# Last batch of the first layer: taken in two halves from the output sums on, one-hot pieces moved behind its rows, landing waits of the stores ahead removed

## The reference, cut to what matters

```python
x = x + 0.5 * L0_ffn(layernorm(x))    # x @ W_base + b, plus the top 2 of 8 low-rank experts, gates by softmax
x = x + L0_attn(layernorm(x))         # 16 heads of 16, LoRA on q, k, v and o
x = x + 0.5 * L0_ffn(layernorm(x))
x = x + 0.5 * L1_ffn(layernorm(x))    # 32 experts, 4 given per token, silu(g) * u, down
x = x + L1_attn(layernorm(x))         # causal, low-rank q and kv, rope
x = x + 0.5 * L1_ffn(layernorm(x))
```

## Time and profile before

| | us |
|---|---|
| median of 3 runs | 1463.39 |
| the profiled execution, its own time | 1460.13 |
| its span, first to last instruction | 1458.3 |
| PE busy | 1262.3 (87%) |
| DVE busy | 952.2 (65%) |
| ACT busy | 670.3 (46%) |
| POOL busy | 491.1 (34%) |

### The profile page before, as it was taken

The page is one execution under the profiler, slowest core; times in us unless marked ns, Lnnn a source line. Parts: engine busy times, 40 slices in busy tenths (PEclk is TensorE's granted clock), DMA queues, the critical chain, the costliest instruction groups (busy, mean ns, idle before and its releaser), DMA issues.

```text
span 1458.3 us, 22406 instructions
## 1 busy us (share of the span) xinstructions
PE 1262.3 (87%) x6657; PEld 824.8 (57%) x6658; DVE 952.2 (65%) x2794; ACT 670.3 (46%) x1700; POOL 491.1 (34%) x493
## 2 busy tenths in 40 slices
PE   6879888898888399998879898889889997799997
PEld 4554243343325388887646455556546655678886
DVE  6796758777778422224698979887897794133334
ACT  2205655556573055553345444553554453255550
POOL 3054040053123645552211211351153143455550
PEclk8989999999999699999999999999999999799999
DMA  8537443065313266544011100020000102355647
GB/s 287 104 36 122 182 87 44 1 120 185 137 37 149 98 230 202 193 154 170 15 44 30 29 1 1 12 105 1 8 33 18 59 33 94 127 189 183 205 138 303
DMA packets 79120, 151.89 MB, mean 104 GB/s; under 512 B 11677, under 2 KB 60254, under 8 KB 75422
## 3 DMA queue, kind: packets, MB, share of 16 engines
q1 hardware_dynamic: 63310, 108.59, 25.8%
q0 software_dynamic: 15264, 41.70, 8.0%
q10 hardware_dynamic: 432, 0.17, 0.0%
HBM read 85.29 MB, written 64.75 MB: 103 GB/s over the span
## 4 chain that ended last, share of the span: by engine, by line
PE 54%; DVE 27%; ACT 6%; issue 6%; POOL 3%; DMA 3%; SPq 0%; DVEq 0%; ACTq 0%; POOLq 0%
PE m_psG L1276 12%; PE m_psY L1292 6%; DVE a_t L1733 5%; DVE a_mx L924 4%; PE a_psA L1490 3%; DVE a_nb L1741 3%; PE a_psO L482 3%; POOL rows_dram L167 3%; PE m_psX L1267 3%; PE a_psU L1469 3%; ACT a_pr L1600 2%; PE a_psU L457 2%; PE a_psU L1478 2%; PE a_psO L1513 2%; DVE a_q L1729 2%
## 5 line engine op out<-in xcount | busy, mean ns | idle before, releaser
L167 POOL DMA_INDIRECT outs_dram<-m_ys,dest x190 | 181.9, 958 | 156.0 <-ACT m_ys L1194 150.8
L1600 ACT ACTIVATE a_pr<-a_psA,a_nb 128x512 f32<-128x512 f32 (+3 forms) x256 | 132.7, 525 | 216.0 <-DVE a_nb L1741 216.0
L1214 DVE TENSOR_TENSOR m_hm<-m_psG,m_sg 128x128 f32<-128x128 f32 x190 | 55.5, 292 | 252.9 <-ACT m_sg L1188 251.8
L924 DVE TENSOR_REDUCE a_mx<-a_psU 128x1 f32<-128x512 f32 x256 | 163.4, 684 | 63.8 <-PE a_psU L457 62.8
L1276 PE MATMUL m_psG<-arena,m_xgT 128*128 x760 | 200.4, 386 | 3.8 <-ACT m_xgT L1182 3.2
L1657 POOL TENSOR_TENSOR a_q<-a_q,a_t 64x512 f32<-64x512 f32 x64 | 80.9, 1263 | 347.4 <-DVEq L1736 325.8
L167 POOL DMA_INDIRECT rows_dram<-a_xd,slot x112 | 114.7, 1024 | 157.2 <-DVE a_xd L147 72.3
L610 ACT ACTIVATE a_P<-a_psS 128x512 f32<-128x512 f32 x256 | 142.6, 597 | 50.4 <-PE a_psS L468 48.2
L1276 PEld LDWEIGHTS m_psG<-arena,m_xgT 128*128 128x128 f32 x760 | 129.8, 191 | 20.5 <-issue 9.1
L1741 DVE TENSOR_REDUCE a_nb<-a_psA 128x1 f32<-128x512 f32 (+3 forms) x256 | 113.3, 485 | 34.3 <-PE a_psA L1492 25.0
L457 PE MATMUL a_psU<-arena 96*128 96x512 bf16 x256 | 101.6, 397 | 27.0 <-DVE a_mx L924 25.5
(11 more groups left out here) (299 smaller groups left out, 2310.3 us busy)
## 6 DMA issues: line engine op xcount, KB each, us to landing
m_xg<-rows_dram SPq DMA_DIRECT2D x46, 512.0 KB, 4.2
arena<-in_mo_w SPq DMA_DIRECT2D x9, 2048.0 KB, 9.3
arena<-part_dram SPq DMA_DIRECT2D x96, 128.0 KB, 5.6
arena<-outs_dram SPq DMA_DIRECT2D x20, 512.0 KB, 3.8
rows_dram<-a_P SPq DMA_DIRECT2D x6, 1024.0 KB, 14.6
part_dram<-a_part SPq DMA_DIRECT2D x16, 384.0 KB, 5.1
rows_dram<-arena SPq DMA_DIRECT2D x6, 1024.0 KB, 13.2
arena<-outs_dram SPq DMA_DIRECT2D x6, 1024.0 KB, 13.4
```

The costliest lines, as they stand in the source:

```text
L167: pool.indirect_dma_start(out=rows_dram, out_offset=bass.IndirectOffsetOnAxis(ap=slot[:, c:c + 1], axis=0), in_=row, in_offset=None).then_ ...
L924: dve.tensor_reduce(mx[g % 2][:, 4 * kt + qt:4 * kt + qt + 1], psU[n % 2][:, :], AX, ALU.max).then_inc(u_free, 1)
L1600: ins = act.activation(pr[S % 2][:, AT[t]:AT[t] + (t + 1) * P], psA[:, AT[t]:AT[t] + (t + 1) * P], ACT.Exp, bias=nb[S % 2][:, t:t + 1], sc ...
```

## The change

The points of i = 5 do nothing any more on TensorE, ScalarE and VectorE; what stood there is written out behind the loop as `last_half_turns`, `last_half_copies` and `last_half_rows`. In words:

1. Batch 3's output sums: at OA VectorE now does for each half `half_rows`: add, stats, scales, two tiles of fxn; before, both adds came first and the rest for all four tiles together.
2. The last FFN: TensorE takes x unit 0, m 0, m 1, x unit 1, m 2, m 3, and then for each half the h transposes (two tiles) and its l unit. VectorE does gate rows 0 and 1, gap and gates of the first half, gate rows 2 and 3, the rows of the first half, then gap and gates of the second half, `block_values(2)`, the rows of the second half.
3. `all_ones(3)` (all four pieces, 8 tensor_tensor in a row) and `block_values(3)` stand behind the last rows. `products(2)` and `products(3)` are behind the last l unit. stay_warm: 3 in place of 7 ahead of x unit 0, 8 in place of 2 ahead of the h unit (of the second half).
4. Batch 2's four landing waits on GpSimd are gone.

The core of the diff (`turn_unit`, `main_unit` and `hidden` hold what stood in the loops before, with the h key carrying its half):

```diff
-            IDLE_LAST = {("ao", B - 1, 0): 3, ("ao", B - 1, 1): 3, ("x", 2, B - 1, 0): 7, ("h", 2, B - 1): 2}
-            INVERT_AT = {("x", 2, B - 1, 0): (0, 1), ("h", 2, B - 1): (2,)}
+            IDLE_LAST = {("ao", B - 1, 0): 3, ("ao", B - 1, 1): 3, ("x", 2, B - 1, 0): 3, ("h", 2, B - 1, 1): 8}
...
+                elif kind == "h":
+                    n, b = key[1:3]
+                    js = tiles_of(key)
+                    pe.wait_ge(h_gated, chain(n, b) + 1 + js[0] // 2)
+                    turn(key, [(psT[0:64, j * P:(j + 1) * P], hid[:, j * 64:(j + 1) * 64]) for j in js])
...
+            def last_half_turns():
+                n, b = 2, B - 1
+                products(0)
+                products(1)
+                turn_unit(("x", n, b, 0))
+                main_unit(("m", n, b, 0))
+                main_unit(("m", n, b, 1))
+                turn_unit(("x", n, b, 1))
+                main_unit(("m", n, b, 2))
+                main_unit(("m", n, b, 3))
+                for u in range(2):
+                    turn_unit(("h", n, b, u))
+                    main_unit(("l", n, b, u))
+                products(2)
+                products(3)
...
+            def last_half_copies():
+                n, b = 2, B - 1
+                for u in range(2):
+                    turned(act, ("x", n, b, u))
+                    act.copy(fxT[:, u * 2 * D:(u + 1) * 2 * D], psT[:, :]).then_inc(t_free, 1)
+                for u in range(2):
+                    for j in (2 * u, 2 * u + 1):
+                        hidden(("m", n, b, j))
+                    act.wait_ge(gap_ready, chain(n, b) + u + 1)
+                    act.activation(ex[:, 2 * u:2 * u + 2], gap[:, 2 * u:2 * u + 2], ACT.Exp).then_inc(ex_ready, 1)
+                    turned(act, ("h", n, b, u))
+                    act.copy(hidT[0:64, 2 * u * P:(2 * u + 2) * P], psT[0:64, 2 * u * P:(2 * u + 2) * P]).then_inc(t_free, 1)
...
-            def last_rows(c):
-                b, two = B - 1, slice(2 * c, 2 * c + 2)
-                add(("l", 2, b, c), b, c)
+            def half_rows(key, u, sc, ready):
+                b, two = B - 1, slice(2 * u, 2 * u + 2)
+                add(key, b, u)
+                released(dve, key)
...
+            def last_half_rows():
+                n, b = 2, B - 1
+                for j in (0, 1):
+                    gate_row(n, b, j)
+                half_gap(0)
+                half_gates(0)
+                for j in (2, 3):
+                    gate_row(n, b, j)
+                half_rows(("l", n, b, 0), 0, sd, xd_ready)
+                half_gap(1)
+                half_gates(1)
+                block_values(2)
+                half_rows(("l", n, b, 1), 1, sd, xd_ready)
+                all_ones(3, range(HC // TOPK))
+                block_values(3)
...
-                if ffn_at(i, p, GM[0]) == (2, B - 1):
-                    block_values(2)
-                    all_ones(3, (0,))
...
-                if ffn_at(i, p, LA) == (2, B - 1):
-                    all_ones(3, (1, 2))
-                    for c in range(2):
-                        last_rows(c)
-                    all_ones(3, (3,))
-                    block_values(3)
-                    return
...
+                    if p == OA and b == B - 1:
+                        turned(dve, ("x", 2, B - 2, 1))
+                        for u in range(2):
+                            half_rows(("p", b, u), u, s2, fn_ready)
+                        return
...
-                if b < B - 1 or hi == TPB * TOPK:
+                if b < B - 2 or b == B - 1 and hi == TPB * TOPK:
                     pool.wait_ge(placed[b % 2], 16 * (b // 2 * TPB * TOPK + hi))
```

More of the change, by code:

```diff
@@ L215, in turn_units @@
             out += [("x",) + ffn_at(i, p, TX) + (u,) for u in range(2)]
-        if ffn_at(i, p, TH):
+        if ffn_at(i, p, TH) == (2, B - 1):
+            out += [("h", 2, B - 1, u) for u in range(2)]
+        elif ffn_at(i, p, TH):
             out.append(("h",) + ffn_at(i, p, TH))
@@ L250, in first_layer @@
     chain = lambda n, b: b + (B if n == 2 else 0)
+    tiles_of = lambda key: range(2 * key[3], 2 * key[3] + 2) if len(key) > 3 else range(TPB)
     with ExitStack() as ctx:
@@ L380, in side @@
             def side(i, p):
+                if i == B + 1:
+                    return
                 for key in turn_units(i, p):
[L382 to L412, removed]
@@ L413, in side @@
-                for key in main_units(i, p):
[L414 to L449, removed]
@@ L532, in _ @@
                 side(i, p)
-            products(QUARTERS - 1)
+            last_half_turns()
         @block.scalar
@@ L539, in _, with hidden @@
                 act.dma_start(dst, src).then_inc(route_in, 16)
+            def hidden(key):
+                _, n, b, j = key
+                act.wait_ge(main_read, TPB * chain(n, b) + j + 1)
+                act.copy(hid[:, j * 64:(j + 1) * 64], bank(key)[:, D + E:NM]).then_inc(free_of(key), 1)
+            def last_half_copies():
[10 more added lines that the diff above has]
+                    act.copy(hidT[0:64, 2 * u * P:(2 * u + 2) * P], psT[0:64, 2 * u * P:(2 * u + 2) * P]).then_inc(t_free, 1)
             def side(i, p):
+                if i == B + 1:
+                    return
                 for key in turn_units(i, p):
@@ L564, in side @@
                     if kind == "m":
-                        _, n, b, j = key
-                        act.wait_ge(main_read, TPB * chain(n, b) + j + 1)
-                        act.copy(hid[:, j * 64:(j + 1) * 64], bank(key)[:, D + E:NM]).then_inc(free_of(key), 1)
+                        hidden(key)
                     elif kind == "qk":
@@ L909, in side @@
                         link(row_stats(dve, r, b))
-                    if p == OSC[0]:
+                    if p == OSC[0] and b < B - 1:
                         scales_begin(dve, link, r, b, s2)
-                    if p == OSC[1]:
+                    if p == OSC[1] and b < B - 1:
                         scales_end(dve, link, s2)
@@ L926, in _ @@
                 side(i, p)
+            last_half_rows()
             invert()
```

117 lines of the change are left out of this document (103 added, 14 removed).

## The result

The changed kernel takes 1479.01 us (median of 4 runs, 1475.98 to 1479.71), the kernel before beside it 1464.1 (4 runs, 1462.01 to 1467.23): the ratio is 1.0097, 95% interval 1.0076 to 1.0117. It is slower by about 1%. The forecast was 1459.7, its range ended at 1464.5, and "slower by over 0.5%" had 3%. The profiled execution has a span of 1474.1 us in place of 1458.3: +15.8; its last scatter starts 16.5 later than before, so what lies behind gave 0.7 back.

The account below looks back on a forecast made before the run. It took GpSimd's 32 scatters of batches 2 and 3 as the bound, VectorE close behind. Earlier batch 3 scatters -4.95, second half +0.6, one-hot pieces +0.7: -3.65 us from 1463.39 gives 1459.7, range 1456.0 to 1464.5.

Parts of the forecast that it names:

- Landing waits: GpSimd, batch 2: without the waits its scatters end at 478.4 to 479.4; from there VectorE's rows decide.
- The 478.4: Forecast end of batch 2's scatters without landing waits, worked as 459.39 + 15 x 1.264.
- Halves: Batch 3's output sums and last FFN in halves: its first scatter starts at 480.3, 4.95 us earlier than 485.25.
- The 1.17: Time from the start of VectorE's rows for batch 3 to the scatter that needs the first: 484.08 to 485.25.
- Second half: Batch 3's ninth scatter, needing the third tile, starts at 491.0, 0.6 us late behind VectorE's rows.
- One-hot pieces: VectorE's eight two-input tensor_tensor from about 490.5 delay batch 3's last eight scatters: +0.7 us, bounds 0 and 3.8.
- the first rival: VectorE's row of one-hot pieces shuts GpSimd out; ninth scatter costs 3.8 more: -0.9 us, 1462.5; chance 20%.
- the small price: Scatters beside the one-hot pieces wait for one instruction each: three at 0.35 less 0.36, +0.7 us.
- the two near rows: Earlier-trace VectorE rows beside the scatters at 478.12 and 490.29, read as costing a scatter 0.36 to 0.50.
- products(3) and dest: After the scatter streak: done at 500.8 against a last landing at about 503.3, hidden by 2.5 us.
- All of VectorE's back-to-back work: Rival: one-hot pieces and `block_values(3)` shut GpSimd out from 490.5 to 497.0: +1.2 us, 1464.6; chance 5%.
- TensorE at the lower level: Rival: lower clock through the halves, units at 2.3, batch 3's first scatter 2.7 later: -1.6 us, 1461.8; chance 12%.

Follow-up runs that it names:

- e1: The changed kernel with batch 2's four landing waits put back, nothing else undone; 1465.11 us, ratio to before 1.0015.
- e5: The changed kernel with two of batch 2's landing waits put back, after 8 and after 16 scatters; 1464.94 us, ratio 1.0029.
- e8: The changed kernel with three GpSimd memsets of 128x512 after each four scatters of batch 2, no landing waits; 1467.16 us, ratio 1.0029.
- e4: The changed kernel with one landing wait of batch 2 put back, after its first four scatters; 1472.42 us, ratio 1.0069.
- e9: e1 with all_ones(3) moved ahead of the rows of the first half; 1465.12 us, ratio 1.0025.
- e7: e1 with a link behind every one-hot tensor_tensor, so VectorE waits for each; timed with 12 runs: 1459.49 us, ratio 0.999.
- e13: The changed kernel with 256 one-column ScalarE copies, waiting for nothing, ahead of its first copy of the last FFN; 1493.84 us (one run).
- e6: The changed kernel with the last 4 MB of expert weights loaded only after batch 2's scatters have landed; 1476.12 us, ratio 1.0106.
- e11: The changed kernel with 64 one-column ScalarE copies, waiting for nothing, ahead of its first copy of the last FFN; 1478.44 us (one run).
- e2: The kernel before with batch 2's four landing waits removed and nothing else changed; 1477.16 us, ratio 1.0102.
- e3: The changed kernel with 64 always fulfilled waits added to ScalarE's stream at i = 1, far ahead of the tail; 1481.87 us, ratio 1.0117.
- e10: e9 with batch 2's landing waits replaced by one-column GpSimd memsets, pauses of some 0.9 us; 1473.77 us, ratio 1.007.

## Why the prediction was wrong

The step that failed is **Landing waits**: it took their removal as a gain only, and asked of it what comes late next on VectorE, but put its effect on TensorE and ScalarE at nothing. In those pauses TensorE caught up and its reports came through (e1, e5, e8). It was worth +17.1 us: the copy of x unit 0 was due at 463.96 (the transposes at 463.3 and their 0.66) and came at 481.29. Of these 17.3 us, 11.8 are TensorE's late semaphore and 5.5 its late transposes (shown as done at 469.46): 0.5 of later start, the rest its slow matmuls. Batch 3's first scatter came at 497.38 and not 480.3. From the copy to it lie 16.1 us, 16.3 by the forecast: the two m units took 4.71 and not 2.92, but they no longer had to wait for VectorE. The line on GpSimd's own side was right: batch 2's scatters ended at 478.61. (The 478.4 is where a scatter behind the sixteenth could start; by the same working the sixteenth ends at 478.05, and the row began 0.53 later.)

**Halves**: right. The adds start at 458.81 and 463.74, the rows 4.26 behind the first (4.25 forecast), the second half's rows end at 468.9 (468.1, with 0.5 of later start). The sum isn't seen in the kernel after, since the stand overlays it, but e1 shows it without the stand: the first half's rows for the experts start 24.8 behind batch 2's first scatter (480.54 less 455.71), 25.35 by the forecast. The 1.17 from such rows to their scatter was misread: in before that scatter was released by a landing, not by VectorE. Where VectorE does release it, it takes 0.69 (496.69 to 497.38, 507.33 to 508.02).

**Second half**: right. The ninth scatter starts 10.64 behind the first, 10.7 forecast.

**One-hot pieces**: wrong in size, and for the reason that the first rival named. The ninth scatter took 5.16 and not 0.96, ending 0.84 after the last of the eight. The row at 508.02 to 521.08 is 13.06 long against 9.9: +3.2, with 17.1 and -0.1 the whole of 521.08 less 500.9. The prediction chose the small price since "a scatter is under way here when the row begins". That premise fails by its own figure: with the third tile 0.6 late, GpSimd stands idle before the ninth scatter. It fails for one of the two near rows as well: when VectorE's row around 478.12 began, at 476.99, GpSimd was in a landing wait. In before at 453.75, after at 454.28 and 508.02 and e4 at 496.41 a scatter began within 0.13 us of the start of VectorE's row after an idle of 0.78 us or more, and was shut out to the row's end. In e5 at 497.58 it began the same 0.04 behind the row's start, but after an idle of 0.37, and lost only 0.52. Those in mid-row lost 0.50 at most (e1, e9, and the earlier trace rows at 478.12, though that one had stood idle for 1.73). Just when a scatter is shut out is thus known for these places and not as a rule. The Trainium skill, SBUF — State Buffer, section "SBUF: two separate sides", has a lock between a GpSimd instruction that reads SBUF and a VectorE one with two SBUF inputs: whichever starts first holds it for that whole instruction. That agrees with e7's 1.65, which ends 0.84 after the first of the eight; of 5.33 and 5.16 it does not account, and the measurement decides.

**products(3) and dest**: right, dest was written at 518.02 to 518.3, the last landing is at 523.5.

**The rivals**: the first one's mechanism is real and came on top of the loss. "All of VectorE's back-to-back work" is wrong: the scatter ended at 513.18, while `block_values(3)` ran from 512.38 to 514.5. "TensorE at the lower level" had 2.3 us for a unit, and the first two m units after the stand took 4.71, but the stand was there already. No rival had it.

**What the trace of before could have told**: only that its rows of scatters were broken every four, where others had work. Batch 3's sixteen without a pause looked like proof of harmlessness; but TensorE had nothing to do beside them until 493.00, and then only 32 matmuls and 16 of stay_warm. In the kernel after, batch 3's row did no harm either, and in e9 it slowed only matmuls that nobody waits for.

**Open**: by what way scatters hold the other engines back. Two readings are left: instructions on the core are handed on late, or finished ones are reported late and the engine stops when too many are unreported. e13 fits both; the late semaphores are seen, and are what cost the time in the kernel after. The DMA engines were at a share of 0.27 to 0.30 only, the late loads have no part in it (e6), and no instruction packet was under way (e13). Why steps of 0.7 us, and how long a row it takes, is not settled either: TensorE's first gap came 8.0 us after the first scatter's start (462.26 in after), VectorE ran 32 instructions there without one and in e4 had its first 12.9 us into the row. The same rows sent from another engine's queue weren't tried.

## To carry to other kernels

A wait can do work that no row shows: before taking pauses out of a long row of DMAs issued by GpSimd, look whether other engines have work beside it, and leave a pause of some 1.7 us every four (e1). With one every eight (e5) the intervals of the two overlap, but the row was 1.9 us longer (53.33 against 51.46). In a trace, gaps put down to "issue" in the middle of independent instructions are the first sign. An idle of many us whose releaser is "remote" in a program on one core was in every case here a semaphore raised long after the instruction that raises it is shown as done: look up when it changed, and on which engine that instruction is. One-column copies that wait for nothing tell whether an engine is slow of its own: they showed that ScalarE was (e13), and that this wasn't what its copy waited for (e11). And a scatter that GpSimd starts from idle just as an unbroken row of two-input VectorE instructions starts can cost the whole row; links between these bring most of it back.

## What the runs showed of the hardware

- Beside scatters 1.26 us apart without a pause ScalarE started one instruction per 0.49 us (36 in 17.75), against one in 0.094 otherwise, though they waited for nothing. TensorE (after) and VectorE (e4) were slowed as well.
- TensorE's semaphore for its transposes came up to 12.3 us after they are shown as done (after 11.8, e2 8.1, e3 12.2, e6 12.3), 2.2 to 3.2 us after the last scatter of the row ended (after 2.7, e2 2.2, e4 3.2). With a landing wait or 2.7 us of memsets after the fourth scatter it came at once (e1, e8); a pause of 0.9 there was not enough (e10).
- Eight VectorE instructions of two inputs without a gap shut out for 4.2 to 4.4 us a scatter that began from idle with the first of them; with gaps of 0.03 us or more the same eight cost it 0.7 (1.65 less 0.96). Other scatters beside such rows lost 0.52 at most.
